# Seven token buffers in turn instead of six in the first FFN stage of a routed four-layer kernel

## The reference

```
h = x @ W_down[role] + b_down[role]          # 512 -> 256
h = gelu(h)
y = x + h @ W_up[role] + b_up[role]          # 256 -> 512, residual
x = layernorm(y) * gamma[role] + beta[role]  # over the 512 features, eps 1e-5
```

## Time and profile before

| | |
|---|---|
| median of 3 runs | 2616.32 us (2616.24 to 2621.03) |
| the profiled execution | 2620.1 us |
| its span, first to last instruction | 2618.4 us |
| TensorE, VectorE, ScalarE, GpSimd busy | 95%, 40%, 35%, 14% |
| mean granted TensorE clock | 0.983 |
| end of the first stage | about 231.6 us into the span |

### The profile page before, as it was taken

One profiled execution on the slowest core, in us unless ns is written; L12 is line 12 of the kernel. 1 busy time (PEld: TensorE's weight loads), 2 busy tenths in 40 slices (PEclk: granted clock), 3 DMA queues, 4 the chain that ended last, 5 costly groups with the idle time before them and its releaser, 6 DMA issues. The chain is left out here.

```text
span 2618.4 us, 29174 instructions
## 1 busy us (share of the span) xinstructions
PE 2477.1 (95%) x11376; PEld 2049.8 (78%) x11376; DVE 1048.2 (40%) x1434; ACT 922.3 (35%) x1242; POOL 377.6 (14%) x294
## 2 busy tenths in 40 slices
PE   5888999999999999999999999998999999969995
PEld 4765788888878888888788888887888888758884
DVE  4544333422244333222433342224333322357776
ACT  3544333322234333222334332223333222246663
POOL 2673000000000000000000000000000000029887
PEclk9999999999999999999999999999999999989997
DMA  5444011021120110211201111102111111063243
GB/s 185 153 169 177 33 48 48 32 80 48 48 81 33 50 46 33 80 48 48 97 33 48 48 71 58 48 32 81 43 41 56 50 48 50 34 225 137 81 137 129
DMA packets 41676, 195.64 MB, mean 75 GB/s; under 512 B 5746, under 2 KB 5746, under 8 KB 24836
## 3 DMA queue, kind: packets, MB, share of 16 engines
q1 hardware_dynamic: 35844, 152.68, 16.8%
q0 software_dynamic: 5760, 41.95, 4.0%
HBM read 163.16 MB, written 31.46 MB: 74 GB/s over the span
## 5 line engine op out<-in xcount | busy, mean ns | idle before, releaser
L1181 DVE TENSOR_TENSOR h_lo<-g,h_hi 128x512 fp32r<-128x512 f32 x256 | 177.4, 693 | 756.3 <-ACT h_hi L1089 756.3
L57 PE MATMUL bank<-h_hi,w_hiB 128*128 128x512 f32 x1152 | 449.2, 390 | 11.7 <-DVE h_lo L1158 11.7
L59 PE MATMUL bank<-h_hi,w_loB 128*128 128x512 f32 x1152 | 448.4, 389 | 0.0
L58 PE MATMUL bank<-h_lo,w_hiB 128*128 128x512 f32 x1152 | 448.2, 389 | 0.0
L1086 ACT ACTIVATE g<-bank,bias_cols 128x512 f32<-128x512 f32 x256 | 176.5, 689 | 630.0 <-PE bank L59 393.2
L59 PE MATMUL bank<-o_hi,w_loA 128*128 128x512 f32 x768 | 298.9, 389 | 0.0
L57 PE MATMUL bank<-o_hi,w_hiA 128*128 128x512 f32 x768 | 298.8, 389 | 0.0
L58 PE MATMUL bank<-o_lo,w_hiA 128*128 128x512 f32 x768 | 298.8, 389 | 0.0
L1028 ACT ACTIVATE w_hiB<-w_raw 128x2048 fp32r<-128x2048 f32 x37 | 71.0, 1920 | 565.5 <-PE bank L59 565.5
L57 PEld LDWEIGHTS bank<-h_hi,w_hiB 128*128 128x128 f32 x1152 | 216.2, 188 | 58.2 <-issue 6.7
L59 PEld LDWEIGHTS bank<-h_hi,w_loB 128*128 128x128 f32 x1152 | 216.2, 188 | 45.5
(11 more groups left out here) (210 smaller groups left out, 4213.8 us busy)
## 6 DMA issues: line engine op xcount, KB each, us to landing
w_raw<-in_units_a SPq DMA_DIRECT2D x32, 1024.0 KB, 4.8
w_raw<-in_units_b SPq DMA_DIRECT2D x32, 1024.0 KB, 4.8
w_raw<-in_units_c SPq DMA_DIRECT2D x16, 1024.0 KB, 4.8
w_raw<-in_w_packed SPq DMA_DIRECT2D x30, 512.0 KB, 4.1
w_raw<-in_rows_packed SPq DMA_DIRECT2D x20, 512.0 KB, 4.5
x_tok<-x SPq DMA_DIRECT2D x16, 512.0 KB, 6.6
x<-stage SPq DMA_DIRECT2D x32, 256.0 KB, 2.8
first_gain<-in_rows_packed SPq DMA_DIRECT2D x10, 512.0 KB, 4.5
```

Of the source, the lines that this page charges most:

```text
L57: pe.matmul(out, lh, rh, start=(i == 0), stop=False)
L58: pe.matmul(out, lh, rl, start=False, stop=False)
L59: last = pe.matmul(out, ll, rh, start=False, stop=(i == len(terms) - 1))
L1181: v.tensor_tensor(h_lo[:, j, cols(n)], g[q % 2][:], h_hi[:, j, cols(n)].bitcast(F32), ALU.subtract).then_inc(hlo_done, 1)
```

## The change

The first stage gets a seventh buffer, and a gather that reuses a buffer waits for the semaphore of the scatter that last emptied this very buffer. With an even number of buffers the parity of j and of j - NX were the same; with seven they are not. The last stage keeps its ten buffers.

```diff
-    NX = NG if NL > 1 else 6
+    NX = NG if NL > 1 else 7
...
                 if j >= NX:
-                    pool.wait_ge(stored[j % 2], 16 * ((j - NX) // 2 + 1))
+                    pool.wait_ge(stored[(j - NX) % 2], 16 * ((j - NX) // 2 + 1))
```

## The result

The median went from 2617.33 us (4 runs, 2616.24 to 2621.03) to 2589.89 us (4 runs, 2587.78 to 2592.76). The ratio is 0.9893 with a 95% interval of 0.9876 to 0.9911, so 23 to 32 us less; forecast were 2589.8 us and a range of 2587 to 2599. The profiled execution took 2590.2 us, with a span of 2588.5.

What follows compares the result with a forecast made beforehand. TensorE, busy 95% of the span, was taken as the bound, so gains come only where it idles or runs at a lower clock. Four steps give 26.5 us: 2616.32 - 26.5 = 2589.8 us, range 2587 to 2599.

Steps and rivals of the forecast that it cites:

- The wait named as the cause: First FFN stage: the gather of group 6 waits on `stored` for a scatter just issued, idling GpSimd 7.28 us.
- The sum: Four slow first-stage steps return to 13.59 us each, 26.5 us off the 80.89 they took.
- Idle time and clock: Of the 26.5 us in four slow steps, 18.4 are TensorE's idle time, 8.1 its loss at the lower clock.
- GpSimd's new step: First FFN stage: GpSimd's step sums to 13.03 us, below TensorE's 13.59; 14.1 with a scatter of 2.11 us.
- The slack: First FFN stage: `rstd_shift` is done 2.0 us before `norm` wants it, enough for 0.5 us a step over four steps.
- Rival A: GpSimd becomes the bound at 15.0 us a step in the four steps, total 2594 to 2600; chance 0.09.
- Transfers: First-stage gathers issued right behind scatters land in 13.5 us by medians, 21.3 at longest, wanted after 18; no loss.
- The bound of 9.4 us: Weight load issued at 94.82, wanted by `split_down` at 100.5, would have to take over 9.4 us to hurt.
- B: Gathers land 3.3 us late in the four steps, losing 3.3 to 13 us, total 2593 to 2603; chance 0.07.
- D: Gather queued behind the scatter lands 7.9 us late in each of four steps, 2622 us or more; chance 0.02.
- Rival C: The gather's issue blocks behind the undrained scatter, the 7.28 us stay, time as before, 2616; chance 0.04.
- The rule of the shared port pair: VectorE operations with two SBUF inputs lock out GpSimd's SBUF reads; one meeting a step gives 14.1 us, within the slack.

Runs made afterwards that it cites:

- the repeat: The changed kernel run again with no edit, beside the kernel before on the same chip: 2590.61 us against 2619.39, ratio 0.9891.
- the memset of half a microsecond: Changed kernel plus a 128x512 GpSimd memset ahead of `rstd_shift` in steps 4 to 7 of the first stage: 2593.84 us, ratio 0.9908.

## Why the prediction was right, step by step

- **The wait named as the cause** was the right one, although the row put it down to TensorE's transposes. With it kept for three of four gathers, three slow steps stayed (22.2 us); one gather freed gave one fast step.
- **The sum** was 26.5 us; the steps gave 26.7, since they run at 13.55 and not 13.59. The medians of before and after on one chip differ by 28.8 us in the repeat, with an interval of 25 to 32 us, which holds 26.7; the 2 us between the two are not resolved, and the steps don't show them.
- **Idle time and clock.** TensorE's waits of 18.4 us are gone, and the lower clock with them (1.00 in all four steps); there was no edit that gave one without the other.
- **GpSimd's new step** was mis-sized: 13.03 us forecast, 13.55 measured from scatter to scatter. Missing were 0.27 us between the scatter and the gather issued behind it (0.30 against the 0.03 I took from other pairs), 0.1 in the gather, which meets the end of the weight split, and 0.1 to 0.15 in the gains. The first gather took 1.80 us for the same reason (start 89.20, a split from 88.95 to 90.14), within the 1.1 us allowed for it. "The gather starting within 0.1 us of the scatter's end" was wrong by 0.2.
- **The slack** was forecast as 2.0 us and is 0.9, as these rows of ScalarE in the changed kernel show:

```profile
89.33 0.19 ACT L489 ACTIVATE first_columns<-first_mean_var 128x4 f32<-128x4 f32 x1
...
93.26 1.51 ACT L494 ACTIVATE first_x<-first_x,first_columns 128x512 f32<-128x512 f32 x2
```

  `norm` starts at 93.26 without waiting, and GpSimd's `rstd_shift` was done at 92.35. It stays at 0.9 in all four steps, as GpSimd's pace equals TensorE's. That is no chance. VectorE's weight split comes once in a step of TensorE's, and the gather behind it ends 0.84 to 0.86 us after the split in each of the four steps (in the repeat too):

```profile
102.50 1.19 DVE L547 TENSOR_TENSOR first_wd_lo<-w_raw,first_wd_hi 128x1024 fp32r<-128x1024 f32 x1
```

  This split ends at 103.69, and the gather at 103.44 + 1.09 = 104.53. Without meeting it the gather takes 0.97 us, so GpSimd's own work is about 13.43 us, an estimate from these rows. "GpSimd has only 0.56 us to spare" was still too kind: it is 0.12. "Then the gathers end and GpSimd catches up" held: its first step without a gather takes 12.53 us, and it waits 1.04 us for ScalarE in the next. Rival A, GpSimd as the bound, was nearer than its 0.09 says; the memset of half a microsecond brings it about.
- **Transfers.** The gathers did land late, 11.5 us after issue (median of four, 5.6 before), near the sum of both medians, 13.5, and well short of the 18 us at which TensorE would wait. Weight loads went from 5.9 to 8.3 us. The bound of 9.4 us for them was misread: the load issued at 92.27 landed at about 100.6, while the `split_down` that was said to want it started at 97.89 without waiting. SyncE issues that load after the low part of group 5 is made, so by the code it is group 7's, and its `split_down` is one step later, at 111.44: some 11 us in hand. Rivals B and D did not occur, and neither came close.
- **Rival C**, a gather whose issue blocks behind the scatter: the longest gather instruction is 1.80 us, and that is the weight split's doing.
- **The rule of the shared port pair** bore out in the main. The Trainium skill, page "SBUF — State Buffer", section "SBUF: two separate sides", calls it an exclusive lock held for a whole instruction. The runs agree in both directions: a split of 1.19 us became 4.04 beside GpSimd's adds, and a scatter of 1.06 became 1.69 behind a split. They show two things more. VectorE didn't get in between two adds issued back to back. And a DMA instruction of GpSimd that starts first neither waits nor holds up the split: the scatter at 102.08 ends at 103.14, 0.64 us into the split, which takes 1.19 us all the same.

## What to carry to other kernels

A buffer is worth what it adds between the release of a place and its next use: here the release was a store issued by the same in-order queue an instant before, so the queue stood still for the store's whole latency, and with it every small instruction behind. Look behind each wait for the small operation that another engine needs; its lateness, not the late transfer, cost the time. Before buying memory, look at where the wait stands in the queue: moving it by 6 us gave four fifths of the gain (21.5 of 26.7 us by the steps), and with it came a new collision that only the timelines of both engines showed.

## What the runs showed of the hardware

- VectorE's operation with two SBUF inputs waits for both of GpSimd's back-to-back adds on SBUF, not just for the one running: 4.04 and 4.32 us in place of 1.19, ending 1.10 us after the second.
- GpSimd's indirect DMA instruction, when it starts after such a VectorE operation, ends 0.84 to 0.95 us behind it: up to 2.14 us in place of 0.97 to 1.06. When the DMA instruction starts 0.03 us or more ahead, neither is longer.
- Two indirect DMAs issued by GpSimd one after the other lie 0.30 us apart, and the second, a megabyte behind a megabyte, lands in 11.5 us where it takes 5.6 to 6.0 with the queue free.
